# Small heads in the second attention: values as 32-column weights, a transposed result, and the exponent per head straight from PSUM

## The chip, the cores and the metric

The kernel runs on one core of a Trainium2 chip. The metric is the device time of one execution in microseconds (us). The kernel before took 516.53 us in the median of three runs (513.0 to 519.35).

## The reference, cut to what matters

The program is a decoder of four gated blocks, each an attention over a context of 128 tokens and a feed-forward part, on a batch of 8 items of 128 tokens by 128 features. Only the second attention (layer A1 in the kernel) changes. It has 16 heads of 8 features:

```
Q = split_heads(x_norm @ w_q.T); K = split_heads(ctx @ w_k.T); V = split_heads(ctx @ w_v.T)
scores = Q K^T / sqrt(8);  scores = where(mask == 0, -1e9, scores)
attn = softmax(scores, axis=-1)          # 16 heads, 128 x 128 each, per item
out  = (attn @ V) -> 128 x 128;  x = x + tanh(g) * (out @ w_o.T + b_o)
```

## The kernel before, in words

**Tiles and layers.** Everything is fp32 in tiles of 128 partitions. The program walks a plan of steps. In the first half of the plan the layers A0 (attention with 16 heads of 64 features), F0 (a quantized feed-forward part), A1 and ROUTE (the router of an expert layer) are in flight together: A0 starts at step 0, F0 at step 4, A1 at step 8, ROUTE at step 12, and each layer takes one new item per step. So F0's last work is in steps 11 to 13, A1 and ROUTE run together in steps 12 to 18, and from step 19 on ROUTE finishes alone. After that come the experts (MOE) and the layers A2, F2, A3, F3. A3 is an attention like A1 and is not changed.

**Order of work.** Each engine has a table `stages` that gives, for each layer, four slots of a step; in a slot stand entries such as `(1, scores, A1, 0)`: the lag in steps behind the item's first step, the function, its arguments. `walk` runs slot 0 of all layers, taking an entry of each in turn, then slot 1 and so on. Each engine executes its own list strictly in that order, and waits on semaphores (`wait`) for what it needs. A PSUM bank is taken with `claim`, which waits for the event in `emptied` that says its previous content has been read.

**A1 for one item** works on four groups g of four heads:

1. `scores` (PE, L817 and L821): adds the mask by a bf16 matmul and the scores of four heads by a 512-column fp32 matmul, which the profile shows as two instructions, into bank g % 2 (`S_BANK`).
2. `shifted` (DVE): row maximum per head (L1214), then scores minus maximum into `prob` (L1218). That second instruction frees the bank.
3. `exps` (ACT, L569): one exponent of 512 columns, in place, with the scale 8^-0.5.
4. `probsT` (PE, L829): four transposes; `probsT_sb` (ACT, L561) copies them to SBUF.
5. `pv` (PE, L847): per head the transposed probabilities are the weights (128 x 128) and 9 columns of `va_1` stream, 8 values and a column of ones that yields the softmax denominator. Each is two instructions, so 8 per group.
6. After all groups `norm` (DVE, L1252 and L1254) divides, `ot` (PE, L899) transposes the 128 x 128 result, `ot_sb` (ACT) copies it, `y` (PE, L905 and L907) multiplies by the output weights, `resid` (DVE, L1197) adds to x.

Before that stand the layer norm (`ln_stats`, `rs` on POOL, `ln`), its transpose `xt` and copy `xt_sb`, and `q` with `q_sb`, which writes the query to `qz` in four copies of 32 partitions. The transposes `xt` and `ot` share bank 6 (`R_BANK[0]`). At the program's start POOL clears constants (L451 to L457), and ACT and DVE wait for five of these (`cleared`).

## Time and profile before

| | us |
|---|---|
| median of three runs | 516.53 (513.0 to 519.35) |
| profiled execution, its own time | 514.63 |
| its span in the trace | 512.8 |
| PE, PEld, DVE, ACT, POOL busy in the span | 430.0, 338.2, 336.4, 275.1, 141.6 |

PE is the matrix engine and PEld its weight load, which overlaps it; DVE is the vector engine, ACT the scalar engine. The span is the stretch from the first to the last recorded instruction; the rest of the execution's time lies around it. A busy time is the sum of an engine's instructions with overlaps counted once. PE's instructions are pipelined: the next one starts before the last one's recorded end, so the cost of one in a row of equal ones is the distance between starts.

### The profile page before, as it was taken

The page shows a single profiled execution, that of the slowest core. Times are in us where ns is not written, and L with a number is a line of the kernel's source. Part 1 is how long each engine was busy: PE and PEld are TensorE (multiplying, and loading weights), DVE is VectorE, ACT ScalarE, POOL GpSimd, SP SyncE. Part 2 cuts the span into 40 slices and gives each one's busy share as a digit, 9 for nine tenths or more (in the row PEclk, how much of TensorE's full clock was granted, in tenths as well). Part 3 has the DMA queues.
Part 4 walks back from the last instruction along what each step waited for, and adds up shares of the span by engine and source line. Part 5 has one row for each costly group of instructions (what it writes and reads, how often), then busy time and mean ns, then how long its engine had stood idle before and what let it go on. Part 6 is the DMA issues. An engine that isn't in the chain of part 4 may idle for free.

```text
span 512.8 us, 8536 instructions
## 1 busy us (share of the span) xinstructions
PE 430.0 (84%) x2872; PEld 338.2 (66%) x2886; DVE 336.4 (66%) x1001; ACT 275.1 (54%) x565; POOL 141.6 (28%) x257
## 2 busy tenths in 40 slices
PE   5799899898897789889996799727779999999733
PEld 4587787787786566667786488515556777777722
DVE  1386876886976867757876122236757677888674
ACT  3343345454455356645562265323877889888553
POOL 3180010010120222204434300078552234442252
PEclk9999999999999999979998699955999999999655
DMA  8970000000000020000000223111000000000000
GB/s 312 411 283 2 1 1 2 1 1 1 1 3 0 1 106 20 1 0 12 12 17 20 88 78 116 43 36 37 11 1 2 2 1 0 2 6 6 7 10 15
DMA packets 8570, 21.41 MB, mean 42 GB/s; under 512 B 1376, under 2 KB 4689, under 8 KB 8401
## 3 DMA queue, kind: packets, MB, share of 16 engines
q1 hardware_dynamic: 7505, 18.78, 10.3%
q0 software_dynamic: 1024, 2.10, 1.4%
q8 instruction: 24, 0.39, 0.3%
q14 instruction: 17, 0.14, 0.1%
HBM read 14.00 MB, written 6.88 MB: 41 GB/s over the span
## 4 chain that ended last, share of the span: by engine, by line
PE 65%; DVE 15%; ACT 7%; issue 6%; POOL 6%; DMA 2%; POOLq 0%; DVEq 0%; ACTq 0%; another core or an unknown queue 0%
PE bank L821 9%; PE bank L847 8%; PE bank L829 7%; PE bank L866 4%; PE bank L843 4%; PE bank L805 3%; PE bank L861 3%; PE bank L984 3%; PE bank L992 3%; PE bank L946 2%; PE bank L957 2%; POOL moe_rows L528 2%; PE bank L935 2%; PE bank L788 2%; DVE prob L1218 2%
## 5 line engine op out<-in xcount | busy, mean ns | idle before, releaser
L1214 DVE TENSOR_REDUCE mx<-bank 128x4 f32<-128x512 f32 x96 | 65.8, 685 | 45.3 <-PE bank L821 29.7
L479 POOL TENSOR_SCALAR rstd<-mv 128x1 f32<-128x1 f32 x48 | 10.1, 211 | 241.7 <-DVE mv L1174 240.3
L561 ACT ACTIVATE probT<-bank 128x512 f32<-128x512 f32 x96 | 56.9, 592 | 34.0 <-PE bank L829 31.7
L569 ACT ACTIVATE prob<-prob 128x512 f32<-128x512 f32 x96 | 60.0, 625 | 25.7 <-DVE prob L1218 25.1
L847 PEld LDWEIGHTS bank<-va,probT 128*128 128x128 f32 x512 | 65.8, 199 | 3.0 <-issue 2.9
L1218 DVE TENSOR_TENSOR prob<-bank,mx 128x512 f32<-128x512 f32 x96 | 65.3, 681 | 1.6 <-PE bank L829 0.3
L829 PE MATMUL bank<-pack,prob 128*128 128x128 f32 x384 | 59.8, 279 | 5.2 <-ACT sg L637 1.4
L847 PE MATMUL bank<-va,probT 128*128 128x9 f32 x512 | 63.8, 252 | 0.3
L829 PEld LDWEIGHTS bank<-pack,prob 128*128 128x128 f32 x384 | 46.7, 147 | 25.5 <-issue 22.2
L821 PE MATMUL bank<-moe_rows,qz 128*128 128x512 f32 x64 | 34.2, 618 | 0.1
L821 PE MATMUL bank<-kz,qz 128*128 128x512 f32 x64 | 32.6, 599 | 1.4 <-issue 1.4
L843 PE MATMUL bank<-va,probT 128*128 128x65 f32 x256 | 32.1, 268 | 0.1
L843 PEld LDWEIGHTS bank<-va,probT 128*128 128x128 f32 x256 | 31.3, 192 | 0.0
L528 POOL DMA_INDIRECT moe_rows<-yrows_d,row_of x16 | 15.8, 985 | 48.4 <-DMA yrows_d<-o_n 44.6
L481 POOL TENSOR_TENSOR rstd<-rstd,minus_half 128x1 f32<-128x1 f32 x48 | 26.9, 560 | 4.0
L561 ACT ACTIVATE qT<-bank 128x512 f32<-128x512 f32 x24 | 14.3, 596 | 17.1 <-PE bank L866 17.0
L561 ACT ACTIVATE xnT<-bank 128x128 f32<-128x128 f32 x32 | 8.7, 273 | 26.7 <-PE bank L788 26.7
L866 PEld LDWEIGHTS bank<-xnT,pack 128*128 128x128 f32 x128 | 16.6, 192 | 6.2 <-issue 5.5
L866 PE MATMUL bank<-pack 128*128 128x128 f32 x128 | 18.1, 285 | 2.9 <-ACT kz L561 2.9
L523 POOL DMA_INDIRECT xrows_d<-xn_all,row_of x16 | 16.3, 1017 | 14.8 <-DVE row_of L1378 12.4
L805 PEld LDWEIGHTS bank<-kz,qT 64*128 64x128 f32 x256 | 15.5, 187 | 6.8 <-issue 6.8
L1189 DVE TENSOR_SCALAR xn<-pack,mv,rstd 128x128 f32<-128x128 f32 x40 | 13.8, 357 | 8.9 <-POOL rstd L481 8.7
(230 smaller groups left out, 944.9 us busy)
## 6 DMA issues: line engine op xcount, KB each, us to landing
yrows_d<-moe_rows SPq DMA_DIRECT2D x2, 1510.0 KB, 19.2
pack<-pack_d SPq DMA_DIRECT2D x5, 512.0 KB, 8.2
pack<-pack_d SPq DMA_DIRECT2D x1, 2112.0 KB, 14.8
expert<-experts_d SPq DMA_DIRECT2D x4, 514.0 KB, 9.2
pack<-experts_d SPq DMA_DIRECT2D x4, 514.0 KB, 4.6
xrows_d<-moe_rows SPq DMA_DIRECT2D x1, 1080.0 KB, 17.9
moe_rows<-xrows_d SPq DMA_DIRECT2D x8, 135.0 KB, 3.0
yrows_d<-o_n SPq DMA_DIRECT2D x8, 135.0 KB, 1.8
```

The costliest lines, as they stand in the source:

```text
L481: pool.tensor_tensor(out, out, minus_half, ALU.pow).then_inc(ev.sem, 1)
L528: pool.indirect_dma_start(y_got[:, b, j, :], None, yrows_d, bass.IndirectOffsetOnAxis(ap=row_of[:, b, j:j + 1], axis=0)).then_inc(y_fetche ...
L561: act.activation(dst, src, ACT.Identity if kw else ACT.Copy, **kw).then_inc(E[layer][name].sem, 1)
L569: act.activation(prob[:, g % 2, :], prob[:, g % 2, :], ACT.Exp, scale=float(DK0 if layer == A0 else DK) ** -0.5).then_inc(E[layer]["probs" ...
L805: mm_ = pe.matmul(bank[S_BANK[a]][:, P * t:P * t + P], qT[rows, it.k, cols], kz[rows, it.k, cols], start=False, stop=(t == 3))
L821: mm_ = pe.matmul(out[:, :], qz[:, it.k, P * g:P * g + P], k4[layer][:, it.b % K4_BUFS[layer], :], start=neg is None, stop=True)
L829: mm_ = pe.transpose(bank[T_BANK[g % 2]][:, P * j:P * j + P], prob[:, g % 2, P * j:P * j + P], ident)
L843: mm_ = pe.matmul(bank[O_BANK[g % 2]][:, VW0 * j:VW0 * j + VW0], probT[:, g % 2, P * j:P * j + P], va0[:, it.k, h, :], start=True, stop=True)
L847: mm_ = pe.matmul(bank[O_BANK[it.k]][:, VW * h:VW * h + VW], probT[:, g % 2, P * j:P * j + P], va[:, bass.ds(it.b, 1), h, :], start=True, ...
L866: mm_ = pe.matmul(out[:, P * t:P * t + P].rearrange("p (a n) -> p a n", a=1), w[:, 512 * c + P * t:512 * c + P * t + P], rhs, start=True, ...
L1214: yield from do(dve.tensor_reduce(m, src, AX.X, ALU.max))
L1218: yield from do(dve.tensor_tensor(prob[:, g % 2, :].rearrange("p (h t) -> p h t", h=GH), src, m.rearrange("p (h a) -> p h a", a=1).to_broa ...
```

## The change

The values of A1 are no longer the streamed operand. They are kept with each head in a field of 32 columns (`VSTEP`; 8 values and 24 zeros), and `pv` loads a window of 32 columns as weights and streams the 128 columns of the transposed probabilities. The window starts 8 g columns early, so that the head's values fall on output rows 8 g to 8 g + 7 of the strip of 32 partitions that belongs to j; the four groups accumulate in one 128 x 128 block of PSUM, which is the result already transposed. The column of ones goes away: the exponent, now four instructions per group that read the scores from PSUM with minus the maximum as bias, gives the denominators by its sum output. The subtraction on DVE goes away, and a small negation of the maxima comes. The query takes over the scale 8^-0.5. `norm1` (DVE) forms the reciprocals spread to 128 columns, `rt` (PE) transposes them, `rt_sb` (ACT) copies them, `scale1` (DVE) multiplies the result by them. The transpose of the result (`ot`) and its copy fall away. The wide values lie in a free half of `kz` and in a new tile `hi_1`, which POOL clears at the start. The rows of the output weights are reordered on the host.

```diff
-        va_1 = sb("va_1", [P, B, H, VW])
+        hi_1 = sb("hi_1", [P, B // 2 * H * VSTEP])
+        kz0 = kz[:, 0, :].rearrange("p (k n) -> p k n", k=2)
+        va_1 = [v.rearrange("p (b h n) -> p b h n", b=B // 2, h=H) for v in (kz[:, 1, :], hi_1[:, :])]
+        for g in range(G):
+            emptied[A1, f"s{g}"] = ("probs", g + 1)
 # POOL
+            pool.memset(kz[:, 1, :], 0.0).then_inc(cleared, 1)
+            pool.memset(hi_1[:, :], 0.0).then_inc(cleared, 1)
 # ACT
+            def exps1(it, g):
+                wait(act, A1, "shifted", it, 2 * g + 2)
+                if g >= 2 or it.rep >= 1:
+                    wait(act, A1, "probsT", it, g - 1)
+                for j in range(GH):
+                    ins = act.activation(prob[:, g % 2, P * j:P * j + P], bank[S_BANK[g % 2]][:, P * j:P * j + P], ACT.Exp,
+                                         bias=mxn[:, g % 2, j:j + 1],
+                                         accum_out=rden[:, it.k, G * j + g:G * j + g + 1])
+                ins.then_inc(E[A1]["probs"].sem, 1)
+            def rt_sb(it):
+                wait(act, A1, "ot", it)
+                evac(xn_all[:, it.b, :], bank[R_BANK[0]][:, 0:P], A1, "ot_sb")
-                A1: [[(2, exps, A1, 3), (2, probsT_sb, A1, 2)],
-                     [(3, ot_sb, A1), (1, exps, A1, 0), (2, probsT_sb, A1, 3)],
-                     [(1, exps, A1, 1), (1, probsT_sb, A1, 0), (0, xt_sb, A1)],
-                     [(1, exps, A1, 2), (1, probsT_sb, A1, 1), (0, q_sb, A1)]],
+                A1: [[(2, exps1, 3), (2, probsT_sb, A1, 2)],
+                     [(1, exps1, 0), (2, probsT_sb, A1, 3)],
+                     [(1, exps1, 1), (1, probsT_sb, A1, 0), (0, xt_sb, A1), None, (2, rt_sb)],
+                     [(1, exps1, 2), (1, probsT_sb, A1, 1), (0, q_sb, A1)]],
 # PE
+                    elif layer == A1:
+                        at = VSTEP * (H * (it.b % (B // 2)) + h) - DK * g
+                        mine = (kz[:, 1, :], hi_1[:, :])[it.b // (B // 2)]
+                        mm_ = pe.matmul(bank[O_BANK[it.k]][VSTEP * j:VSTEP * j + VSTEP, 0:P], mine[:, at:at + VSTEP],
+                                        probT[:, g % 2, P * j:P * j + P], start=(g == 0), stop=(g == G - 1))
+            def rt(it):
+                wait(pe, A1, "norm", it, 1)
+                claim(it, A1, "ot")
+                pe.transpose(bank[R_BANK[0]][:, 0:P], xn_all[:, it.b, :], ident).then_inc(E[A1]["ot"].sem, 1)
-                A1: [[(1, scores, A1, 0), (2, probsT, A1, 2), (2, pv, A1, 1), (3, ot, A1)],
+                A1: [[(1, scores, A1, 0), (2, probsT, A1, 2), (2, pv, A1, 1)],
                      [(1, scores, A1, 1), (2, probsT, A1, 3), (2, pv, A1, 2), (3, y, A1)],
-                     [(1, scores, A1, 2), (1, probsT, A1, 0), (2, pv, A1, 3), (0, xt, A1)],
+                     [(1, scores, A1, 2), (1, probsT, A1, 0), (2, pv, A1, 3), (0, xt, A1), (2, rt)],
 # DVE
+            def shifted1(it, g):
+                wait(dve, A1, "scores", it, g + 1)
+                do = chain(A1, "shifted", it, 2 * g)
+                src = bank[S_BANK[g % 2]][:, :].rearrange("p (h t) -> p h t", h=GH)
+                yield from do(dve.tensor_reduce(mx[:, g % 2, :], src, AX.X, ALU.max))
+                if g >= 2 or it.rep >= 1:
+                    wait(dve, A1, "probs", it, g - 1)
+                yield from do(dve.tensor_scalar(mxn[:, g % 2, :], mx[:, g % 2, :], -1.0, None, ALU.mult), hold=False)
+            def norm1(it):
+                wait(dve, A1, "probs", it)
+                dve.reciprocal(xn_all[:, it.b, :].rearrange("p (h n) -> p h n", h=H), rden[:, it.k, :].rearrange(
+                    "p (h a) -> p h a", a=1).to_broadcast([P, H, DK])).then_inc(E[A1]["norm"].sem, 1)
+            def scale1(it):
+                wait(dve, A1, "ot_sb", it)
+                wait(dve, A1, "pv", it)
+                dve.tensor_tensor(oT[:, it.k, 0:P], bank[O_BANK[it.k]][:, 0:P], xn_all[:, it.b, :], ALU.mult
+                                  ).then_inc(E[A1]["norm"].sem, 1)
-                A1: [[[(1, shifted, A1, 0), (0, ln_stats, A1)]],
-                     [[(1, shifted, A1, 1), (0, ln, A1)], (3, resid, A1)],
-                     [(1, shifted, A1, 2)],
-                     [[(1, shifted, A1, 3), (2, norm, A1)]]],
+                A1: [[[(1, shifted1, 0), (0, ln_stats, A1)], (2, norm1)],
+                     [[(1, shifted1, 1), (0, ln, A1)], (3, resid, A1)],
+                     [(1, shifted1, 2)],
+                     [(1, shifted1, 3), (2, scale1)]],
```

## Rows read from the trace of the kernel before

**Rows 1.** The page: busy times, PE in 40 slices, chain by engine.
```profile
PE 430.0 (84%) x2872; PEld 338.2 (66%) x2886; DVE 336.4 (66%) x1001; ACT 275.1 (54%) x565; POOL 141.6 (28%) x257
...
PE   5799899898897789889996799727779999999733
...
PE 65%; DVE 15%; ACT 7%; issue 6%; POOL 6%; DMA 2%; POOLq 0%; DVEq 0%; ACTq 0%; another core or an unknown queue 0%
```
**Rows 2.** Busy time by stretch, steps 11, 12 and 14: stretch, length, engines, PE's clock.
```profile
195.90:209.70 13.80, 11.99 (x80) 9.00 (x80) 11.07 (x31) 8.46 (x20) 2.59 (x5) 1.00 0.00 1
209.70:224.80 15.10, 12.67 (x81) 9.42 (x80) 10.88 (x27) 8.19 (x19) 2.83 (x5) 0.94 0.00 1
...
238.10:248.80 10.70, 10.70 (x75) 8.40 (x74) 8.42 (x26) 6.40 (x15) 4.48 (x8) 1.00 0.04 13
```
**Rows 3.** Timeline of PE in step 14: start us, length, instruction, count.
```profile
239.16 0.38 PE L817 MATMUL bank<-neg,identb 128*128 128x512 bf16 x1
239.38 1.02 PE L821 MATMUL bank<-moe_rows,qz 128*128 128x512 f32 x2
...
240.38 0.63 PE L829 MATMUL bank<-pack,prob 128*128 128x128 f32 x4
240.85 0.96 PE L847 MATMUL bank<-va,probT 128*128 128x9 f32 x8
241.66 0.31 PE L899 MATMUL bank<-pack,o_n 128*128 128x128 f32 x1
```
**Rows 4.** Timeline of PE in a step of A0: a tiled run and its neighbours.
```profile
100.77 1.06 PE L866 MATMUL bank<-xnT,pack 128*128 128x128 f32 x8
101.67 1.00 PE L843 MATMUL bank<-va,probT 128*128 128x65 f32 x8
...
105.98 0.59 PE L797 MATMUL bank<-neg,identb 128*128 128x512 bf16 x2
106.50 1.16 PE L805 MATMUL bank<-kz,qT 64*128 64x128 f32 x16
107.60 0.39 PE L935 MATMUL bank<-t_upT,xqT 128*128 128x512 bf16 x1
```
**Rows 5.** Timeline of ACT: an exponent with bias and sum, then copies.
```profile
378.70 0.37 ACT L601 ACTIVATE va<-bank,va 128x128 f32<-128x128 f32 x1
378.96 0.19 ACT L601 ACTIVATION_READ_ACCUMULATOR va<-bank,va 128x1 f32 x1
379.06 1.50 ACT L561 ACTIVATE qz<-bank,pack 32x128 f32<-32x128 f32 x4
```
**Rows 6.** Groups by line on ACT and DVE: count, busy us, mean ns.
```profile
L569 ACT ACTIVATE prob<-prob 128x512 f32<-128x512 f32 x96 | 60.0, 625 | 25.7 <-DVE prob L1218 25.1
L1218 DVE TENSOR_TENSOR prob<-bank,mx 128x512 f32<-128x512 f32 x96 | 65.3, 681 | 1.6 <-PE bank L829 0.3
L1241 DVE RECIPROCAL rden<-bank 128x4 f32<-128x4 f32 x32 | 5.7, 178 | 17.6 <-PE bank L843 17.6
L1252 DVE RECIPROCAL rden<-bank 128x16 f32<-128x16 f32 x16 | 3.9, 243 | 1.1 <-PE bank L847 1.1
```
**Rows 7.** Timeline of step 11: ACT's exponents and copies, DVE's chain of F0.
```profile
199.01 0.69 ACT L561 ACTIVATE hid<-bank,qs 128x512 f32<-128x512 f32 x1 [0.55 <-PE bank L935]
199.60 0.62 ACT L569 ACTIVATE prob<-prob 128x512 f32<-128x512 f32 x1
...
200.54 0.66 DVE L1293 SCALAR_TENSOR_TENSOR hid<-sg,hid 128x512 f32<-128x512 f32 x1
...
201.48 0.69 DVE L1214 TENSOR_REDUCE mx<-bank 128x4 f32<-128x512 f32 x1 [0.28 <-PE bank L821]
...
205.40 0.14 DVE L1283 TENSOR_SCALAR qs<-qs 128x1 f32<-128x1 f32 x1
```
**Rows 8.** The chain that ended last, in step 11: start us, length, link.
```profile
208.35 0.68 ACT hqT L561
209.03 0.52 ACT prob L569
209.55 0.61 ACT sg L623
```
**Rows 9.** Timeline of the start: POOL's last clearing, and the first data.
```profile
2.18 2.66 POOL L457 MEMSET moe_rows<- 128x3072 f32 x1
```

More of the change, by code:

```diff
@@ L62 @@
 TERNARY = ["gateT", "upT", "downT", "fcT", "projT", "w1T", "w2T"]
+VSTEP = 32
 class Item:
@@ L215, in build @@
         kT_1 = sb("kT_1", [P, B, P])
-        kT_3 = sb("kT_3", [P, B, P])
-        va_1 = sb("va_1", [P, B, H, VW])
+        hi_1 = sb("hi_1", [P, B // 2 * H * VSTEP])
+        kT_3 = hi_1[:, 0:N].rearrange("p (b t) -> p b t", b=B)
         va_3 = sb("va_3", [P, B, H, VW])
@@ L256, in build @@
         mx = sb("mx", [P, 2, GH])
+        mxn = sb("mxn", [P, 2, GH])
         rden = sb("rden", [P, 2, H])
@@ L453, in _ @@
                 pool.memset(va0[:, k, :, DK0:VW0], 1.0).then_inc(cleared, 1)
-            for va in (va_1, va_3):
-                pool.memset(va[:, :, :, DK:VW], 1.0).then_inc(cleared, 1)
+            pool.memset(kz[:, 1, :], 0.0).then_inc(cleared, 1)
+            pool.memset(hi_1[:, :], 0.0).then_inc(cleared, 1)
+            pool.memset(va_3[:, :, :, DK:VW], 1.0).then_inc(cleared, 1)
             pool.memset(qz[:, :, :], 0.0).then_inc(cleared, 1)
@@ L578, in k_sb @@
                 wait(act, A0, "kps", it, c + 1)
-                evac(kz[:, it.k, 512 * c:512 * c + 512], bank[R_BANK[0]][:, :], A0, "k_sb")
+                evac(kz0[:, it.k, 512 * c:512 * c + 512], bank[R_BANK[0]][:, :], A0, "k_sb")
             def q_sb0(it, c):
@@ L589, in q_sb @@
                     mine = slice(GH * DK * g, GH * DK * g + GH * DK)
-                    kw = dict(bias=col["bq_3"][mine]) if layer == A3 else {}
+                    kw = dict(bias=col["bq_3"][mine]) if layer == A3 else dict(scale=float(DK) ** -0.5)
                     evac(qz[mine, it.k, P * g:P * g + P], bank[R_BANK[1]][mine, 0:P], layer, "q_sb", **kw)
@@ L686, in kv_sb @@
                 else:
-                    act.activation(va[:, half, :, 0:DK], bank[c][:, :].rearrange("p (b h n) -> p b h n", b=4, h=H),
+                    dst = va[:, half, :, 0:DK] if n else va[c % 2][:, :, :, 0:DK]
+                    act.activation(dst, bank[c][:, :].rearrange("p (b h n) -> p b h n", b=4, h=H),
                                    ACT.Copy).then_inc(kv_act, 1)
@@ L732, in _ @@
             act.wait_ge(prep_dve, 1)
-            act.wait_ge(cleared, 5)
+            act.wait_ge(cleared, 6)
             prepare()
@@ L804, in row_scores0 @@
                         rows = slice(64 * a, 64 * a + 64)
-                        mm_ = pe.matmul(bank[S_BANK[a]][:, P * t:P * t + P], qT[rows, it.k, cols], kz[rows, it.k, cols],
+                        mm_ = pe.matmul(bank[S_BANK[a]][:, P * t:P * t + P], qT[rows, it.k, cols], kz0[rows, it.k, cols],
                                         start=False, stop=(t == 3))
@@ L844, in pv @@
                                         va0[:, it.k, h, :], start=True, stop=True)
+                    elif layer == A1:
[3 more added lines that the diff above has]
+                                        probT[:, g % 2, P * j:P * j + P], start=(g == 0), stop=(g == G - 1))
                     else:
-                        va = va_1 if layer == A1 else va_3
                         mm_ = pe.matmul(bank[O_BANK[it.k]][:, VW * h:VW * h + VW], probT[:, g % 2, P * j:P * j + P],
-                                        va[:, bass.ds(it.b, 1), h, :], start=True, stop=True)
+                                        va_3[:, bass.ds(it.b, 1), h, :], start=True, stop=True)
                 mm_.then_inc(E[layer]["pv"].sem, 1)
@@ L905, in y @@
                 pe.matmul(out, ones, col[f"bo_{n}"], start=True, stop=False)
-                wait(pe, layer, "ot_sb", it)
+                wait(pe, layer, "norm" if layer == A1 else "ot_sb", it)
                 pe.matmul(out, oT[:, it.k, mine_of(layer)], col[f"woT_{n}"], start=False, stop=True).then_inc(E[layer]["y"].sem, 1)
@@ L1024, in kv3 @@
                     if c < 2:
-                        wait(pe, A1, "shifted", last)
+                        wait(pe, A1, "probs", last)
                     else:
@@ L1118, in piece_name @@
                     return args[0]
-                return {xt_e: "xt", down: "y", y_back: "yb", places: "places", y0: "y", q: "q", ot: "ot", y: "y", scores2: "s", probsT2: "t", pv2: "pv", ht: "ht",
+                return {xt_e: "xt", down: "y", y_back: "yb", places: "places", y0: "y", q: "q", ot: "ot", rt: "ot", y: "y", scores2: "s", probsT2: "t", pv2: "pv", ht: "ht",
                         y_ffn: "y", logits: "lg"}[fn]
@@ L1481, in prepare @@
                                          ALU.mult, ALU.min).then_inc(prep_dve, 1)
-                dve.wait_ge(cleared, 5)
+                dve.wait_ge(cleared, 6)
                 dve.wait_ge(gates_ready, 1)
```

2 lines of the change are left out of this document (1 added, 1 removed).

## The prediction

> **What bounds the kernel now.** I read the page first: PE is busy for 430.0 of 512.8 us and holds 65% of the chain that ended last, DVE 15%, ACT 7% [rows 1]. That is an average, so the stage of the change was read next, step by step. A1 shares steps 9 to 12 with F0 and steps 13 to 16 with ROUTE. The reader should see two regimes [rows 2]. In step 14 PE is busy 10.70 of 10.70 us and ACT 6.40: PE alone sets the step. In steps 11 and 12 PE is busy 11.99 of 13.80 and 12.67 of 15.10 us; nothing is full there, and the step is a chain through PE, DVE and ACT [rows 7, 8]. A change that moves work from DVE to ACT and recasts PE's work has to be priced in both.
>
> **PE: the eight instructions of a group's `pv`.** Before, they take from 240.85 to 241.66, 0.81 us, or 0.10 each: the load of 128 columns of weights sets that pace, not the 9 streamed columns [rows 3]. After, each streams 128 columns of fp32. At full array that is the pace of L866, eight in 0.90 us (100.77 to 101.67), 0.11 each [rows 4]. So without overlap the swap gains nothing. But the four heads go to four strips of columns. The trace has one case of a divided array, L805, where two strips of 64 rows alternate: 16 instructions of the same 128 streamed columns in 1.16 us, the last recorded 0.285 long, so 0.058 apart [rows 4]. Two instructions per head must follow each other in one strip, and instructions start in order, so four strips give the same picture as two: pair by pair, half the time. I take 0.058 x 8 = 0.47 us. The division has a price at its edges: L797 streams until 106.40 (2 x 0.21), L805 starts at 106.50; it streams until 107.43, the next whole-array instruction starts at 107.60: 0.10 + 0.17 = 0.27 us [rows 4]. A group costs 0.74 us, 0.07 less than now; over 32 groups 2.2 us. Bounds: no overlap of column strips 8 x 0.11 + 0.27 = 1.15 us (32 x 0.34 = 11 us more), full overlap of four strips 2 x 0.11 + 0.27 = 0.49 (32 x 0.32 = 10 us less).
>
> The Trainium skill (TensorEngine Tiling (Array Packing), Performance Considerations) recommends exactly this swap of stationary and streaming operand with column tiling, at up to 4x for 32; its Tiling Modes section says that changing the mode drains the engine. The edge gaps above agree with the second; the 4x would be the low bound, and it is the first rival.
>
> `rt` takes the place of `ot`, one transpose of 128 columns for another; zero. But it stands right behind `xt` in slot 2 and both use bank 6, so `rt` must wait until ACT has copied `xt`.
>
> **ACT: the exponent.** The nearest row is L601, a 128x128 exponent from PSUM with bias and sum: it starts at 378.70, its accumulator read at 378.96, the next instruction at 379.06: 0.36 us each [rows 5]. A group takes 4 x 0.36 = 1.44 us, where one of 0.625 stood, which in a row with others costs 0.52 [rows 6, 8]: 0.92 more, 3.7 us per item, 29 us in all eight. It is the same operation, so the bounds are narrow (0.30 to 0.45 each). `rt_sb` replaces `ot_sb`, zero; the scaled `q_sb` stays a copy of the same shape, zero. ACT in step 14 goes from 6.40 to 10.1 us of work, against PE's 10.70 - 4 x 0.07 = 10.4: two engines nearly full at once, each waiting in order on the other.
>
> **DVE.** It loses 4 x 0.681 us per item, at a pace of 0.60 [rows 6], and gets four negations of 128x4. The nearest is 0.14 for 128x1 [rows 7]; with the hold behind the reduce I take 0.25. `norm1` is a reciprocal of 128 columns. From 4 to 16 columns the time grows 65 ns, 5.4 ns a column [rows 6], which gives 0.243 + 112 x 5.4 ns = 0.85 us; low bound 0.28, as if it streamed like a plain operation. Net -2.4 + 1.0 + 0.6 = -0.8 us of work. `scale1` is like the multiply of `norm`. DVE is not full in either regime, so only its place in the chain counts.
>
> **Waits.** The score bank is now freed by the exponent, not by the subtraction. From maximum to probabilities it was 0.60 + 0.63; it is 0.25 + 1.44, 0.5 us longer, and `scores` g + 2 stands behind it on PE, with `probsT` and `pv` behind that. `norm1` in DVE's slot 0 waits for the exponent of group 3 in ACT's slot 0, and behind it on DVE stands slot 1: F0's `hid0`, which is on the chain, the next maximum and `ln`.
>
> **Steps 10 to 12 (with F0).** In step 11 the copy `up_sb` ends on ACT at 199.60 and the exponent of group 3 follows [rows 7]. It will end at 201.05, `norm1` at about 201.95, and F0's first `hid` then starts at 202.0 in place of 200.54; `scores` 1 starts at 201.1, so its maximum comes near 202.65, not 201.48: 1.2 us later. The subtraction gone from the chain gives back 0.5. So F0's quantized rows come 0.7 later, `hqT` too. Then on the chain hqT, prob, sg [rows 8] the exponent of 0.52 becomes 1.44: 0.9. Together 1.6 us a step, three steps, 4.8 us. Step 9 has only the last term without `norm1`: 0.9 - 0.4 = 0.5.
>
> **Steps 13 to 16 (with ROUTE).** I walked one step from the start of `scores` 0. PE: scores 1.08, logits 0.2, transposes 0.44, pv 0.74, at 2.45; slot 1 (scores, transposes, pv, y, places) ends at 5.3. ACT: rest of the query copies 0.87 and exponent 3 end at 2.3, copy 2.8, exponent 0 4.25, copy 4.75, exponent 1 6.2, so no bank is late so far. Slot 2 on PE: scores and transposes end at 6.95, pv and `xt` at 7.75. ACT copies the transposes until 7.65, `xt` until 8.2; `rt` can start only then (PE idle 0.4), its copy ends at 8.8, and exponent 2, behind it, runs until 10.25; copy 10.75, first query copy 11.05. The next step starts there: 11.05 in place of 10.70, and with a hand-over or two not counted 11.2. Four steps, 2.0 us.
>
> **Tail and start.** Behind the last `pv` the transpose and its copy fall away (0.31 [rows 3] and a copy of about as much), 0.6 us less in step 17. At the start POOL clears 2 x 2048 columns more; 3072 take 2.66 us [rows 9], so 3.5 us. The constants that ACT waits for are then ready near 5.6 us, when the first data land anyway; the 3072 columns end near 8.2, in front of SP's store that starts at 7.4, whose data are wanted only by the router. Zero; if that cover were gone, 0.1 to 1.
>
> **Sum.** 4.8 + 0.5 + 2.0 - 0.6 = +6.7 us on the profiled execution's 514.63: 521.3. The median of the runs stands 1.9 above that execution; I put the forecast between, at 522.
>
> **Rivals.**
>
> 1. *Full overlap of four strips, and PE stays the only bound.* Then every group saves 0.32 us: 516.5 - 10 = 506. For: PE sets step 14 alone. Against: pairs in one strip must follow one another, and ACT's 10.1 us of step 14 allow hardly 0.6 us of gain. Chance 0.12.
> 2. *Slower by more: column strips do not overlap.* L805 divides rows, where each strip reads its own partitions; here all strips stream different data over the same 128 partitions. Place: `pv`, 32 times. Price 8 x (0.11 - 0.058) = 0.42 us a group, 13 us where PE counts, some 10 with the slack of steps 10 to 12: 532. It decides as soon as starts inside `pv` are 0.1 apart. Chance 0.18.
> 3. *The longer exponent falls into ACT's idle time.* ACT idles 13.80 - 8.46 = 5.3 us in step 11 and 4.3 in step 14 [rows 2]; if order lets it, only PE's 2.2 us remain, minus: 514. Against: the chain names ACT's exponent in step 11 [rows 8]. Chance 0.15.
>
> The forecast has 0.55, its own range 514 to 530 (a reciprocal of 0.28 us takes 2 off, exponents at 0.30 or 0.45 move it by 6 either way over the chain's steps, and a step at PE's lower clock, such as the 0.94 of step 12 [rows 2], adds some).
>
> **Numbers.** A change of 2% (506.2 or 526.9) is about what can be told from none. Faster: 0.10 of rival 1 and 0.02 of rival 3, 0.12. Slower: 0.17 of rival 2 and 0.13 of the forecast's upper end, 0.30. Within: 0.58. The range 507 to 534 holds all but the low tail of rival 1 and the ends.
>
> **What would show it.** In the trace after: `pv` starts 0.06 apart (0.03 for rival 1, 0.11 for rival 2) and gaps of some 0.27 around them; four exponents of 0.36 each; the reciprocal near 0.85; step 14 at 11.2 with both PE and ACT above 90%; PE idle before `rt`; step 11 at 15.4, with `hid` behind `norm1`. What would make it wrong: the wait of `norm1` hidden, since the exponent of group 3 came earlier; or the clock of PE falling in steps that now have gaps, which would cost several us at once.

## The result, and the profile after

The changed kernel takes 518.5 us in the median of 19 runs (516.26 to 522.28), the kernel before 514.35 us (511.11 to 520.35) in as many on the same chip: a ratio of 1.0086, 95% interval 1.0062 to 1.011. It is slower by 0.9%, some 4.4 us, and lies within 2%. The forecast was 522, its working +6.7 us.

First the page of the changed kernel, as in [rows 1]: busy times, PE and its clock in 40 slices, the chain by engine.

```profile
PE 423.0 (82%) x2872; PEld 316.1 (61%) x2886; DVE 326.1 (63%) x1001; ACT 300.9 (58%) x789; POOL 143.6 (28%) x258
...
PE   5799899889887878688886699827779999999733
...
PEclk9999999999999898989998599965899999999755
...
PE 56%; DVE 17%; ACT 13%; issue 7%; POOL 5%; DMA 2%; another core or an unknown queue 0%; POOLq 0%; DVEq 0%; ACTq 0%
```

PE lost 7.0 us of work and DVE 10.3, and ACT gained 25.8. The chain lost PE (65% to 56%) and took up DVE and ACT. The kernel does less matrix work in more time (its span is 3.8 us longer), so PE stands idle for some 11 us more.

Next the busy times by stretch of the changed kernel. A stretch is a step, from one `q` to the next: steps 9 to 14. [Rows 2] has steps 11, 12 and 14 of before.

```profile
159.48:179.55 20.07, 16.05 (x100) 12.08 (x100) 11.67 (x39) 11.94 (x41) 2.66 (x5) 0.93 0.00 1
179.55:197.27 17.72, 14.19 (x95) 8.97 (x96) 10.50 (x31) 12.01 (x48) 2.48 (x5) 0.89 0.29 91
197.27:211.89 14.62, 10.80 (x80) 6.22 (x80) 9.47 (x29) 11.29 (x47) 2.48 (x5) 1.00 0.00 0
211.89:228.13 16.24, 12.03 (x80) 6.72 (x79) 9.40 (x26) 11.75 (x49) 2.48 (x5) 0.89 0.01 2
228.13:239.27 11.14, 9.78 (x79) 5.90 (x78) 7.12 (x28) 9.16 (x42) 4.66 (x7) 1.00 0.04 13
239.27:250.42 11.15, 9.77 (x76) 5.70 (x75) 7.13 (x26) 9.38 (x45) 4.53 (x7) 1.00 0.04 13
```

And the same view of the kernel before, steps 10 and 13:

```profile
179.70:195.94 16.24, 13.52 (x96) 10.68 (x96) 11.05 (x30) 8.28 (x19) 2.59 (x5) 1.00 0.27 99
...
224.77:238.13 13.36, 13.36 (x79) 10.54 (x78) 8.79 (x28) 6.24 (x15) 4.65 (x7) 0.81 0.02 6
```

In step 14 PE was busy all 10.70 us; now 9.77 of 11.15. The following table puts one profiled execution of each kernel side by side. "Next part" is the start of the first 128x512 projection behind A1 and the router (L1009 before, L1042 after), from PE's timeline; "tail" is what lies between step 15 and it.

| us | before | after | difference | forecast |
|---|---|---|---|---|
| up to the end of step 9 | 179.70 | 179.55 | -0.15 | +0.5 |
| steps 10 to 12 | 45.07 | 48.58 | +3.5 | +4.8 |
| steps 13 to 15 | 34.77 | 33.43 | -1.3 | +1.5 |
| tail | 26.64 | 28.68 | +2.0 | -0.1 (+0.5 - 0.6) |
| next part starts at | 286.18 | 290.24 | +4.06 | +6.7 |

Behind that point the two take 226.6 and 226.4 us, so the whole difference lies ahead of it. The -1.3 is one step: step 13 of before took 13.36 us at a granted clock of 0.81 and busy throughout, against 11.14 at 1.00. Steps 14 and 15 are 0.44 us longer each.

PE's timeline of the changed kernel in step 14, to set beside [rows 3]:

```profile
241.95 0.43 PE L872 MATMUL bank<-probT,hi 128*32 128x128 f32 x8
242.69 0.39 PE L841 MATMUL bank<-neg,identb 128*128 128x512 bf16 x1 [0.32 <-ACT prob L586]
...
244.30 0.42 PE L872 MATMUL bank<-probT,hi 128*32 128x128 f32 x8
244.66 0.49 PE L938 MATMUL bank<-pack 128*128 128x128 f32 x2
...
248.77 0.30 PE L927 MATMUL bank<-pack,xn_all 128*128 128x128 f32 x1 [0.46 <-ACT xnT L570]
248.91 0.38 PE L841 MATMUL bank<-neg,identb 128*128 128x512 bf16 x1
```

All eight instructions of `pv` lie inside 0.42 us, and the next instruction follows 0.36 us after the first (244.30 to 244.66). Before it was 0.81, and the working took 0.74. The same view, ended at 244.43, shows which of them start together:

```profile
244.30 0.32 PE L872 MATMUL bank<-probT,hi 128*32 128x128 f32 x4
```

Four have started by then, and they end within 0.32 us though each lasts 0.30. The single records give the starts as 0, 7, 13 and 20 ns, then 133, 140, 147 and 153 ns. Since instructions in one strip start 0.109 us apart (the first experiment), this is one instruction in each of the four strips and then the second one in each. All 32 groups of the trace show this pattern; in the last two, in the tail at a low clock, the second round comes after 215 ns. PE really is relieved by 0.45 us a group, 14 us in all. It pays them back as waits: for the exponent, because that now frees the score bank (0.32), and for `rt` behind `xt` (0.46).

The groups of the new instructions on ACT and DVE in the changed kernel, steps 9 to tail:

```profile
L586 ACT ACTIVATE prob<-bank,mxn 128x128 f32<-128x128 f32 x128 | 45.3, 376 | 13.6 <-DVE mxn L1263 13.5
L586 ACT ACTIVATION_READ_ACCUMULATOR prob<-bank,mxn 128x1 f32 x128 | 27.7, 216 | 0.0
...
L1267 DVE RECIPROCAL xn_all<-rden 128x128 f32<-128x128 f32 x8 | 7.6, 946 | 4.6 <-ACT prob L586 4.5
```

In a row the exponents start 0.34 to 0.35 us apart, four in 1.4 us. The reciprocal takes 0.95 us.

The chain of waits of the changed kernel in step 11, as in [rows 8]:

```profile
200.68 1.50 ACT prob L586 x8
...
202.21 0.95 DVE xn_all L1267
203.16 0.39 DVE hid L1347
...
209.88 0.50 ACT hqT L570
...
210.79 1.25 ACT prob L586 x7
212.03 0.31 ACT sg L646
```

And the chain in the tail of the changed kernel:

```profile
270.49 1.36 ACT prob L586 x7
271.86 0.62 ACT probT L570
272.47 1.40 ACT prob L586 x8
273.90 0.95 DVE xn_all L1267
...
275.31 0.25 DVE topi L1414 x2
275.70 1.09 PE bank L853 x4
```

In step 11 the last group's exponent, the reciprocal and F0's `hid` follow each other, as the working had it. In the tail the same pair, exponent then reciprocal, stands ahead of the router's `choose` (its `topi`). PE, which before went on to these transposes without a gap, waits, and does its last work at a lower clock (0.71 granted from 274 to 278 us): from the first of four transposes to the next instruction it is 1.02 us instead of 0.44. The wait is in PE's timeline:

```profile
275.70 1.09 PE L853 MATMUL bank<-pack,prob 128*128 128x128 f32 x4 [2.37 <-DVE topi L1414]
```

### The profile page after: what moved, and what is told of

The parts are those of the page before. It is cut to its first block, busy times and chain, and to the rows that moved or that the text cites. A ratio compares the mean times of both kernels' runs of the same rounds, so it can differ in the third digit from the quotient of the medians.

```text
span 516.6 us, 8793 instructions
## 1 busy us (share of the span) xinstructions
PE 423.0 (82%) x2872; PEld 316.1 (61%) x2886; DVE 326.1 (63%) x1001; ACT 300.9 (58%) x789; POOL 143.6 (28%) x258
## 3 DMA queue, kind: packets, MB, share of 16 engines
q1 hardware_dynamic: 7505, 18.78, 10.3%
## 4 chain that ended last, share of the span: by engine, by line
PE 56%; DVE 17%; ACT 13%; issue 7%; POOL 5%; DMA 2%; another core or an unknown queue 0%; POOLq 0%; DVEq 0%; ACTq 0%
PE bank L845 7%; PE bank L853 5%; PE bank L894 4%; PE bank L875 4%; ACT prob L586 4%; PE bank L867 4%; PE bank L829 3%; PE bank L889 3%; PE bank L1017 3%; PE bank L1025 3%; PE bank L979 2%; PE bank L968 2%; PE bank L990 2%; POOL moe_rows L537 2%; PE bank L904 1%
## 5 line engine op out<-in xcount | busy, mean ns | idle before, releaser
L586 ACT ACTIVATE prob<-bank,mxn 128x128 f32<-128x128 f32 x128 | 45.3, 376 | 13.6 <-DVE mxn L1263 13.5
L1251 DVE TENSOR_TENSOR prob<-bank,mx 128x512 f32<-128x512 f32 x64 | 43.9, 686 | 1.3 <-PE bank L853 0.3
L578 ACT ACTIVATE prob<-prob 128x512 f32<-128x512 f32 x64 | 39.9, 623 | 5.6 <-DVE prob L1251 5.4
L845 PE MATMUL bank<-moe_rows,qz 128*128 128x512 f32 x64 | 35.8, 643 | 0.8 <-ACT qz L570 0.8
L875 PEld LDWEIGHTS bank<-va,probT 128*128 128x128 f32 x256 | 33.4, 199 | 3.0 <-issue 2.9
L875 PE MATMUL bank<-va,probT 128*128 128x9 f32 x256 | 32.1, 253 | 0.3
L867 PEld LDWEIGHTS bank<-va,probT 128*128 128x128 f32 x256 | 31.3, 192 | 0.0
L586 ACT ACTIVATION_READ_ACCUMULATOR prob<-bank,mxn 128x1 f32 x128 | 27.7, 216 | 0.0
```

The costliest lines, as they stand in the source:

```text
L578: act.activation(prob[:, g % 2, :], prob[:, g % 2, :], ACT.Exp, scale=float(DK0 if layer == A0 else DK) ** -0.5).then_inc(E[layer]["probs" ...
L586: ins = act.activation(prob[:, g % 2, P * j:P * j + P], bank[S_BANK[g % 2]][:, P * j:P * j + P], ACT.Exp, bias=mxn[:, g % 2, j:j + 1], acc ...
L845: mm_ = pe.matmul(out[:, :], qz[:, it.k, P * g:P * g + P], k4[layer][:, it.b % K4_BUFS[layer], :], start=neg is None, stop=True)
L867: mm_ = pe.matmul(bank[O_BANK[g % 2]][:, VW0 * j:VW0 * j + VW0], probT[:, g % 2, P * j:P * j + P], va0[:, it.k, h, :], start=True, stop=True)
L875: mm_ = pe.matmul(bank[O_BANK[it.k]][:, VW * h:VW * h + VW], probT[:, g % 2, P * j:P * j + P], va_3[:, bass.ds(it.b, 1), h, :], start=True ...
L1251: yield from do(dve.tensor_tensor(prob[:, g % 2, :].rearrange("p (h t) -> p h t", h=GH), src, m.rearrange("p (h a) -> p h a", a=1).to_broa ...
```

## The experiments

**Do the strips overlap, and was that all of PE's gain?** All heads of a group go to strip 0, with each product written over the last instead of accumulated.

```diff
-pe.matmul(bank[O_BANK[it.k]][VSTEP * j:VSTEP * j + VSTEP, 0:P], mine[...], probT[...], start=(g == 0), stop=(g == G - 1))
+pe.matmul(bank[O_BANK[it.k]][0:VSTEP, 0:P], mine[...], probT[...], start=True, stop=True)
```

> The kernel after with all heads of a group written to the first strip of 32 partitions, without accumulation (the result is left wrong: three quarters of it are never written), so that the eight instructions can't overlap across strips. If the 0.35 us of a group come from four strips at once: eight instructions about 0.11 apart, 0.86 us and the edges, 0.5 us more a group; steps 14 and 15 go from 11.15 to about 12, the time 5 to 12 us above the kernel after. If they come from the small weights alone: 0.35 us a group as before, no change from the kernel after.

Measured: 523.56 us, ratio 1.0158 (1.011 to 1.0207). PE's timeline of this kernel in step 14, and the stretch:

```profile
243.47 1.06 PE L872 MATMUL bank<-probT,hi 128*32 128x128 f32 x8
244.46 0.39 PE L841 MATMUL bank<-neg,identb 128*128 128x512 bf16 x1
```

```profile
240.37:252.81 12.44, 11.98 (x76) 8.21 (x75) 7.07 (x26) 9.61 (x45) 4.55 (x7) 1.00 0.03 11
```

The next instruction follows after 0.99 us instead of 0.36. Same instructions, same shapes, another strip: the overlap of the four strips is worth 0.63 us a group. The eight starts are 0.109 us apart here, each behind the last. The step is 1.3 us longer, not 2.5, since a part went into waits that PE has anyway. This kernel is the world of the second rival, column strips that don't overlap: 523.56 us where the rival said 532, and only 0.7% above the changed kernel (four runs, and the two intervals nearly touch).

**The exponent by itself.** The kernel before with `exps1` and `shifted1` alone; the sums go to a tile that nobody reads.

```diff
+                    ins = act.activation(prob[:, g % 2, P * j:P * j + P], bank[S_BANK[g % 2]][:, P * j:P * j + P], ACT.Exp,
+                                         bias=mxn[:, g % 2, j:j + 1], accum_out=sums1[:, it.k, G * j + g:G * j + g + 1])
-                A1: [[(2, exps, A1, 3), (2, probsT_sb, A1, 2)],
+                A1: [[(2, exps1, 3), (2, probsT_sb, A1, 2)],
```

> The kernel before with the new exponent alone (four exponents per group from PSUM with bias and sum, negated maxima on DVE); values product and normalization as before. Theory A (the exponent costs the chain 0.9 us in steps 9 to 12 and, with PE at its full 10.7 us of work in steps 13 to 16, every wait for a bank shows): 5 to 10 us above the kernel before (ratio 1.01 to 1.02), more than the whole change. Theory B (it falls into ACT's idle time): ratio 0.995 to 1.002.

Measured: 510.72 us, ratio 0.9935 (0.9903 to 0.9966). The part that I had priced as the loss is a small gain, below both ranges that I had given. The stretch of step 14 in this kernel:

```profile
236.65:247.31 10.66, 10.66 (x75) 8.46 (x74) 6.59 (x26) 9.40 (x45) 4.53 (x7) 1.00 0.05 15
```

ACT went from 6.40 to 9.40 us, PE is still busy without a gap, and DVE has 1.8 us less to do. While PE sets the step, the longer exponent is free. In steps 10 to 12 it is not: they take 46.53 us against 45.07, step 10 of them at a clock of 0.91. Step 11 ran at full clock in both kernels, and there the exponent alone costs 0.70 us (14.47 against 13.77):

```profile
197.22:211.69 14.47, 12.13 (x81) 8.99 (x81) 8.49 (x31) 11.78 (x49) 2.96 (x5) 1.00 0.00 0
```
 Where all of the 0.65% comes from I can't say: in the trace 2.5 us are step 13, which here ran at full clock (10.89 against 13.36), and 2.3 us lie in stages behind (224.3 us after 226.6), which the edit doesn't touch.

**The same question inside the changed kernel.** One exponent of 512 columns per group from PSUM, with the first head's bias and without sums; the reciprocal and its transpose stay.

```diff
-                for j in range(GH):
-                    ins = act.activation(prob[..., P * j:P * j + P], bank[...][:, P * j:P * j + P], ACT.Exp, bias=mxn[:, g % 2, j:j + 1], accum_out=...)
+                ins = act.activation(prob[:, g % 2, :], bank[S_BANK[g % 2]][:, :], ACT.Exp, bias=mxn[:, g % 2, 0:1])
```

> The exponent of a group is one instruction of 512 columns from PSUM with the bias of the group's first head and without sums; the path of the normalization stays. So ACT gives back 1.40 - 0.6 = 0.8 us a group. Theory (the chain through normalization ends the steps, and the exponent is a link of it in steps 10 to 12 and in the tail): 0.8 us in each of steps 10 to 12, some 0.4 in each of 13 to 15, 1 to 1.6 in the tail, 5 to 7 us less, ratio 0.995 to 0.999. Rival (ACT's longer exponent is in idle time, the normalization alone costs): at most 1.5 us less, ratio 1.005 to 1.009.

Measured: 510.61 us, ratio 0.988 (0.9824 to 0.9935), more than either side had expected. The stretches of steps 12 and 14 in it:

```profile
210.31:224.18 13.87, 10.65 (x80) 6.12 (x79) 9.11 (x26) 8.47 (x19) 3.05 (x5) 1.00 0.01 1
...
234.60:245.02 10.42, 9.84 (x75) 5.60 (x74) 7.12 (x26) 6.67 (x15) 4.53 (x7) 1.00 0.05 17
```

Against the changed kernel: steps 10 to 12 -3.5 us, steps 13 to 15 -0.7 each, tail -2.3, the next part at 281.81 instead of 290.24. So the same four exponents that cost nothing beside the old PE work are 2% here by the ratios. A part of that is the clock: steps 10 and 12 of the changed kernel ran at 0.89 and here at 1.00 (step 11 the other way round, 1.00 and 0.89), and runs at like clock, in the part on the prediction, give some 6 us, 1.2%. At full clock in both traces stand the 0.7 us of each of steps 13 to 15. With `pv` at 0.36 us and the normalization waiting for their end, PE no longer covers the exponents.

**The path of the normalization, taken out.** The same edit on two kernels: on the changed one, and on one that has the new `pv` with the old subtraction and exponent. There the denominators are missing; this second base is the first run below, and the two after it also leave the division out. (`...` stands for entries that don't change.)

```diff
-                A1: [[[(1, shifted1, 0), (0, ln_stats, A1)], (2, norm1)],
+                A1: [[[(1, shifted1, 0), (0, ln_stats, A1)]],
-                     [..., (0, xt_sb, A1), None, (2, rt_sb)],
+                     [..., (0, xt_sb, A1)],
-                     [..., (0, xt, A1), (2, rt)],
+                     [..., (0, xt, A1)],
-                dve.tensor_tensor(oT[:, it.k, 0:P], bank[O_BANK[it.k]][:, 0:P], xn_all[:, it.b, :], ALU.mult
+                dve.tensor_tensor(oT[:, it.k, 0:P], bank[O_BANK[it.k]][:, 0:P], ones, ALU.mult
```

> The kernel after with the old softmax back (maximum and subtraction on DVE, one exponent of 512 columns per group on ACT) and the new values product kept. It leaves the softmax denominators out: the reciprocal is taken of old numbers. Theory A (the values product now costs PE 0.35 us a group where it cost 0.81, 15 us in all, and what eats that gain is the exponent): steps 13 to 16 fall from 10.7 to about 9.2 us, steps 10 to 12 by about 0.5, and the time is 6 to 10 us below the kernel before (ratio 0.98 to 0.988). Theory B (the swap itself gains nothing, because the steps are chains and not PE's work): ratio 0.995 to 1.005.

> e1 without the normalization path: no reciprocals, no transpose rt, no copy rt_sb; the product is multiplied by ones, so the division by the denominators is left out. The swap alone in e1 took 1.2% more than the kernel before although PE's product fell from 0.81 to about 0.4 us a group. Theory C (the new normalization path, with its 0.95 us reciprocal on DVE and its hand-overs through bank 6, is what the swap pays with): steps 14 and 15 fall from 11.3 to about 9.3 us, and the time is 5 to 10 us below the kernel before (ratio 0.98 to 0.99). Theory D (the divided array is what costs, by its mode changes and by PE's lower clock in steps 9 to 12): steps 14 and 15 fall, steps 9 to 12 stay at 17 us with a clock of 0.8 to 0.9, ratio 1.00 to 1.01.

> The kernel after without the normalization path (no reciprocals, no rt, no rt_sb; multiplied by ones, the division is left out); exponents with their sums kept. Theory C: the waits of PE behind the copy of xt (0.46 and 0.61 us a step) and of DVE behind the exponent of group 3 go, steps 14 and 15 fall from 11.15 to about 10 (ACT's 9.4 us of work are then the floor), the ratio to the kernel before is 0.985 to 0.995. Theory D: ratio 1.00 to 1.01.

| | with the path | without | the path |
|---|---|---|---|
| new `pv`, old exponent | 1.0124 (1.0076 to 1.0173) | 0.9876 (0.9834 to 0.9918) | 2.5% |
| new `pv`, new exponent | 1.0086 (1.0062 to 1.011) | 0.984 (0.98 to 0.9879) | 2.5% |

The first of these kernels took 522.20 us, 1.2% more than before: neither of my two theories for it came (0.98 to 0.988, 0.995 to 1.005). The other two took 509.43 and 507.49 us, as the theory of the path had it, and against the rival that the divided array itself costs; only step 14 fell less than I had said (to 10.55 and 10.41 us, not 9.3 and 10). Three instructions, a reciprocal, a transpose and a copy, 1.5 us of work per item, cost 11 to 13 us over eight items. Both rows say the same, so it doesn't hang on the exponent's form. In the traces of the second row the next part starts 11.7 us earlier: 3.1 us of that are step 10, 0.5 step 11, 2.5 step 12, 2.2 steps 13 to 15 and 3.5 the tail. Step 12 is mostly clock: it ran at 0.89 with the path and 1.00 without. Both kernels without the path also had the higher clock over their whole runs (0.917 to 0.933 against 0.899 to 0.920); whether the path brings the lower clock is not shown. The stretches of steps 11 and 14 in the changed kernel without the path:

```profile
194.29:208.42 14.13, 10.56 (x80) 6.12 (x79) 8.36 (x30) 11.61 (x48) 2.97 (x5) 1.00 0.00 1
...
232.54:242.95 10.41, 9.46 (x74) 5.54 (x73) 6.71 (x25) 9.12 (x44) 4.54 (x7) 1.00 0.06 20
```

Step 14 gives back 0.74 us, as with the single exponent (0.73): in slot 2 ACT's exponent and the hand-over of `rt` follow each other, and either one gone frees the same time. The tail is 25.22 us instead of 28.68.

**Place or length of the reciprocal?** First `norm1` a slot later, then the reciprocal taken of 16 columns and spread by a copy, then both.

```diff
-                A1: [[[(1, shifted1, 0), (0, ln_stats, A1)], (2, norm1)],
-                     [[(1, shifted1, 1), (0, ln, A1)], (3, resid, A1)],
+                A1: [[[(1, shifted1, 0), (0, ln_stats, A1)]],
+                     [[(1, shifted1, 1), (0, ln, A1)], (3, resid, A1), (2, norm1)],
```

```diff
-                dve.reciprocal(xn_all[...], rden[...].to_broadcast([P, H, DK])).then_inc(E[A1]["norm"].sem, 1)
+                dve.reciprocal(rden[:, it.k, :], rden[:, it.k, :]).then_inc(E[A1]["norm"].sem, 1)
+                dve.wait_ge(E[A1]["norm"].sem, E[A1]["norm"].at(it, 1))
+                dve.tensor_copy(xn_all[...], rden[...].to_broadcast([P, H, DK])).then_inc(E[A1]["norm"].sem, 1)
```

> The kernel after with the reciprocal (norm1) moved on DVE from the end of slot 0 to the end of slot 1, behind F0's first hidden operation and the next maximum. If norm1, which waits for the exponent of group 3 and then takes 0.95 us, holds back F0's chain in steps 10 to 12: 2 to 4 us less than the kernel after (ratio to the kernel before 1.001 to 1.005). If the maximum behind it waits for the same exponent through its bank anyway: no change from the kernel after (1.007 to 1.011).

> The reciprocal is taken of the 128x16 denominators and spread to 128 columns by a copy, so that norm1 should hold DVE for some 0.24 + 0.25 with a hold between, 0.55 to 0.6 us, in place of 0.95. Theory (the length of norm1 ahead of hid0 and, in the tail, ahead of choose is on the path): up to 0.35 to 0.4 us in each of steps 10 to 12 and once an item in the tail, 1.5 to 3 us less than the changed kernel, ratio 1.003 to 1.006. Rival (only its wait for the exponent of group 3 counts, not its length): no difference, ratio 1.008 to 1.010.

> The same short reciprocal, and norm1 behind slot 1 instead of slot 0 of DVE. Theory: the gains of the two add as far as they touch the same steps; norm1 a slot later gave 0.5%, and its length then stands ahead of fewer things, so ratio 0.999 to 1.003. Rival (once norm1 stands behind hid0 its length is in DVE's idle time): the same as norm1 one slot later alone, 1.003 to 1.005.

Measured: later 1.0038 (1.001 to 1.0067), short 0.9976 (0.9939 to 1.0012), both 1.0 (0.9964 to 1.0036). The place came as the first theory had it. Shortening an instruction of 0.95 us is worth 1.1%, more than I had expected, and moving it behind as well adds nothing that the intervals show. DVE's timeline in step 11 of the kernel with the short reciprocal:

```profile
201.21 0.25 DVE L1267 RECIPROCAL rden<-rden 128x16 f32<-128x16 f32 x1 [1.03 <-ACT prob L586]
201.50 0.23 DVE L1269 COPY xn_all<-rden 128x128 f32<-128x128 f32 x1
201.64 0.68 DVE L1349 SCALAR_TENSOR_TENSOR hid<-sg,hid 128x512 f32<-128x512 f32 x1
```

`hid` starts 0.43 us after the reciprocal, not 0.95. The stretches of steps 10 to 12 there:

```profile
179.09:195.78 16.69, 12.49 (x98) 8.05 (x97) 9.45 (x32) 12.33 (x51) 2.84 (x5) 1.00 0.30 97
195.78:210.09 14.31, 10.85 (x82) 6.22 (x80) 8.85 (x32) 11.80 (x49) 2.84 (x5) 1.00 0.00 0
210.09:224.04 13.95, 10.64 (x80) 6.11 (x79) 8.11 (x27) 11.37 (x48) 2.70 (x5) 1.00 0.01 2
```

Step 11, at full clock in both traces, is 0.31 us shorter: that is the length on the chain. Steps 10 and 12 are 1.0 and 2.3 us shorter, and PE is busy 1.7 and 1.4 us less in them for the same instructions: in the changed kernel they ran at a clock of 0.89. So most of the gain in this pair of traces is the clock. How much of it is in the 1.1% of the timed runs stays open, since the runs' own clocks by step aren't recorded; runs at like mean clock, below, give 0.6%. The tail stays at 28.56, but it ran at a granted clock of 0.73 against 0.81 of the changed kernel, so it can't be read for the length. PE's wait in it did get shorter, 1.99 us instead of 2.37:

```profile
271.79 1.09 PE L853 MATMUL bank<-pack,prob 128*128 128x128 f32 x4 [1.99 <-DVE topi L1416]
```

The place counts for more: with `norm1` a slot later `choose` runs ahead of the reciprocal, the wait is 0.59 us, and the tail is 26.20, with both edits 25.81 (at clocks of 0.85 and 0.84).

**Can the order of `rt` be mended?** `rt` ahead of `xt` on PE, and its copy ahead of `xt_sb` on ACT.

```diff
-                     [(1, exps1, 1), (1, probsT_sb, A1, 0), (0, xt_sb, A1), None, (2, rt_sb)],
+                     [(1, exps1, 1), (1, probsT_sb, A1, 0), None, (2, rt_sb), (0, xt_sb, A1)],
-                     [(1, scores, A1, 2), (1, probsT, A1, 0), (2, pv, A1, 3), (0, xt, A1), (2, rt)],
+                     [(1, scores, A1, 2), (1, probsT, A1, 0), (2, pv, A1, 3), (2, rt), (0, xt, A1)],
```

> The transpose rt stands ahead of xt on PE, and its copy ahead of xt_sb on ACT. Theory (the hand-over through bank 6 costs PE 0.46 us per step before rt, since rt waits for the copy of xt): rt no longer waits for ACT, xt waits for the copy of rt instead, so steps 13 to 15 stay within 0.3 us of 11.15; the two share one bank in either order, and the ratio stays 1.006 to 1.011. Rival (the wait is one of order alone and can be removed by order): steps 13 to 15 fall to 10.7, ratio 1.003 to 1.005.

Measured: 1.0112 (1.0076 to 1.0148). PE's timeline in step 14:

```profile
252.58 0.30 PE L927 MATMUL bank<-pack,xn_all 128*128 128x128 f32 x1 [0.62 <-ACT xnT L570]
253.34 0.30 PE L812 MATMUL bank<-pack,xn 128*128 128x128 f32 x1 [0.46 <-ACT xn_all L570]
```

The wait of 0.46 us has changed its owner, and step 14 stays at 11.16. The ratio lies just above the upper end of what I expected; in its trace step 10 ran at a clock of 0.83 and took 20.41 us. Two results through one bank and one copying engine wait for each other in either order.

**Denominators without the path.** The old way got them as a ninth streamed column for nothing. In the new layout they can come from PE too: behind each product a second one with a 32-column window of ones (8 ones, 24 zeros) as weights gives the denominator of the head already on its 8 rows, so nothing has to be spread or transposed. DVE then takes one reciprocal of a 128 x 128 block and multiplies. Both blocks accumulate in one bank, which a bf16 product with zeros clears first.

```diff
+                        pe.matmul(bank[O_BANK[it.k]][:, 0:2 * P], identb[:, :], zerob[:, :], start=True, stop=False)
...
+                        mm_ = pe.matmul(bank[O_BANK[it.k]][VSTEP * j:VSTEP * j + VSTEP, P:2 * P], ones8[:, 24 - DK * g:24 - DK * g + VSTEP],
+                                        probT[:, g % 2, P * j:P * j + P], start=False, stop=(g == G - 1))
...
+                yield from do(dve.reciprocal(rinv[:, it.k, :], bank[O_BANK[it.k]][:, P:2 * P]))
```

> A complete kernel: the new values product, the old softmax path, and the denominators from PE, by a second product per head with a window of ones as the 32-column weights and the same streamed probabilities, so that they come already spread over the result's layout; no transpose of reciprocals and no copy of it. Theory A: a group's two products cost PE about 0.57 us against 0.81, and two of the waits go; the 128-column reciprocal of 0.95 us stands on DVE behind the last product. 4 to 8 us below the kernel before (ratio 0.984 to 0.992). Theory B (only the chain through ACT and DVE counts): ratio 0.995 to 1.005.

> A complete kernel: e5 (new product, denominators by a window of ones on PE) with the new exponent from PSUM, without its sums. e2 and e5 alone stand at 0.9935 and 0.9986 of the kernel before. If the two gains add up because they are on different engines (DVE loses the subtraction, PE 0.12 us a group): 0.985 to 0.993, below e2. If PE's lower clock in the steps with gaps takes it back: 0.995 to 1.005.

Measured: with the old subtraction and exponent 514.59 us, 0.9986 (0.995 to 1.0023); with the new exponent, without sums, 508.15 us, **0.9847 (0.9813 to 0.9881)**. The first came as its theory B had it, with steps 11 and 12 at clocks of 0.89 and 0.90; the second at the lower end of the gain that I had expected. It computes all that the reference asks and beats both kernels; its steps 9 to 15 all ran at full clock in the trace. Its step 14, PE's timeline, one group's exponents on ACT, and the stretch:

```profile
235.99 0.45 PE L880 MATMUL bank<-probT,hi 128*32 128x128 f32 x8
236.23 0.42 PE L882 MATMUL bank<-probT,ones 128*32 128x128 f32 x8
236.58 0.39 PE L847 MATMUL bank<-neg,identb 128*128 128x512 bf16 x1
```

```profile
236.74 1.14 ACT L593 ACTIVATE prob<-bank,mxn 128x128 f32<-128x128 f32 x4
```

```profile
233.18:243.38 10.20, 10.20 (x108) 6.50 (x107) 7.57 (x26) 8.06 (x26) 4.54 (x7) 1.00 0.05 16
```

Both products of a group take 0.59 us, still less than the 0.81 of before. PE is busy throughout again and the waits are gone. ACT has 8.06 us instead of 9.38: the copy of `rt` is worth 0.26 of that (9.12 us in the changed kernel without the path), and the rest is the accumulators that are no longer read, four exponents in a row taking 1.14 us, not 1.40.

## Why the prediction was right, and by which of its steps

The sign, the size class and two of the mechanisms held. The sum was 2.6 us above what the profiled executions show (+4.06 up to the next part), and that nearness is luck in part: a gain of 14 us of PE's work was not foreseen, most of it went into waits that the working had not counted either, and the clock moved single steps by 2 us in both kernels.

**`pv` on PE: the saving was wrong by a factor of six.** I gave a group 0.74 us, 0.07 less than before; it takes 0.36, 0.45 less. The step that failed is "four strips give the same picture as two: pair by pair, half the time". The second instruction of a head doesn't hold up the next strip: four instructions start within 20 ns, so one in each of the four strips, and the four second ones from 133 ns on. Eight in one strip start 0.109 us apart, so a round of four strips costs about what one instruction costs, and the pace is the 2 x 0.11 of the full-overlap bound. The rest, 0.36 - 0.22 = 0.14 us by that estimate, is the edges; I had read 0.27 from another pair of shapes, and so even the bound of full overlap, 0.49, stood above the measurement. The Trainium skill (TensorE: Matmul & The Clock Gate, Part 3: Packing small matmuls) states that matmuls placed in different tiles of the array run at the same time, with about 4 ns of issue for each further tile. The trace agrees with the overlap; between starts in neighbouring strips it shows 7 ns.

**The first rival's price was right and its condition wrong.** The full overlap came, 14 us of PE, but "PE stays the only bound" didn't: PE was down to 9.77 of 11.15 us. The time it named, 506, is near where the kernels without the path of the normalization lie (509.43, 507.49 and 508.15).

**The exponent: right length, account right in part.** 1.40 us a group against 1.44. Exchanged alone, subtraction and exponent cost 0.70 us in step 11, at full clock on both sides; the working's term for a step with the exponent and without `norm1` was 0.5 (step 9), so that charge was about right. Yet the whole kernel with this exchange got 0.65% shorter, and no run says where all of that comes from. What the working had wrong is the place of the larger price. In the changed kernel the four are dear, 1 to 2% above a single one, in steps 13 to 15 (0.7 us each) and the tail too, for a reason that it held only in part: PE's cover was gone, by the very 0.45 us that I hadn't seen.

**Normalization in the steps with F0: the mechanism as forecast, the size too large.** In step 11 the exponent of group 3 ends at 202.18; the working had 201.05 in a step that began 1.3 us earlier, which is 202.4. Then comes the reciprocal, then `hid`. The reciprocal took 0.95 us, not 0.85. The step was to be 15.4 us, 1.6 more than before, and is 14.62, 0.85 more. Step 11 is also the one step of the three that ran at full clock in both kernels, and four kernels at full clock split its 0.85: the exponent +0.70, the path +0.49 (14.62 against 14.13), and the new `pv`, by difference, -0.34. The 3.5 us of the three steps looks nearer to the forecast 4.8 than that, but steps 10 and 12 of the changed kernel ran at a clock of 0.89, so that nearness is not the working's merit. Left out, the path gives 2.5% by the ratios: it is more than the whole loss, and most of it lies outside step 11, in step 10, in the hand-over of steps 13 to 15 and in the tail.

**Steps with ROUTE: right.** The walk gave 11.2, with PE idle for 0.4 us before `rt` and exponent 2 behind the copy of `rt`. The trace has 11.15, 0.46 us and that order. Of "PE and ACT above 90%" neither came (88% and 84%), since `pv` was shorter and ACT's work 9.4 us instead of 10.1. Over the whole stretch the trace shows a gain, because step 13 of before ran at a clock of 0.81; I had used step 14 for all four and not looked at what step 13 held.

**Tail: wrong sign.** I took off 0.6 us for the transpose and copy that fall away, and 2.0 were added. What the working left out is that the pair which it had found ahead of `hid`, exponent and reciprocal, stands once more ahead of the router's `choose` when the last items drain and nothing covers it. The tail is 26.37 us with one exponent per group and 26.20 with `norm1` one slot later. With the short reciprocal it is 28.56, at a lower clock, though PE waits 0.38 us less.

**The clock.** I had named a lower clock in steps with gaps as a risk. In the trace steps 9, 10 and 12 ran at 0.93, 0.89 and 0.89 where before only step 12 was below 1.00 (0.94). But it is not settled as an effect of the change: through step 9 the kernels with another place or length of the reciprocal and with another order of `rt` issue the same instructions as the changed one. With the reciprocal short or a slot later, or `rt` first, that step took 18.64 to 18.65 us at 1.00; in the changed kernel it took 20.07 at 0.93, and with the reciprocal both short and later 20.24 at 0.92. Between single executions a step can differ by that much.

The lower clock is therefore a rival for every ratio above. It can be held against the timed runs, whose mean clocks over the whole execution are on record. Among those at 0.915 to 0.918 the changed kernel has a median of 518.35 us (nine runs), the kernel before 514.07 (20 runs beside the experiments), the short reciprocal 515.24 (three) and the single exponent 512.01 (three). So at like clock the change still costs 4.3 us; the length of the reciprocal is worth 3.1 us (0.6%, where its theory had 1.5 to 3 us) and the four exponents 6.3 us (1.2%), where the ratios say 1.1 and 2%. These are few runs, and the mean doesn't fix the time: four runs of the changed kernel took 520.6 to 520.81 us at 0.919 and three others 516.26 to 517.93 at 0.920.

## What to carry to other kernels

When a change takes work from the engine that sets the time, ask first what that work had been covering: here 14 us came off PE, and the exponent, which had been free beside it, and a new reciprocal became the bound. Price a small instruction by what stands behind it in its queue and not only by its length, in the last items of a loop above all; before a ratio of 1% is put down to an edit, compare the granted clocks on both sides; and keep a by-product such as a softmax denominator in the layout in which it will be used, even at the price of one more product on PE.

## What the runs showed of the hardware

- Eight fp32 instructions with 32 columns of weights and 128 streamed columns, two in each of four column strips, occupy PE for 0.36 us; in one strip 0.99 us. Sixteen take 0.59 us. At full clock the first ones of the four strips start 7 ns apart and the second ones 0.13 us after them.
- A reciprocal on DVE takes 0.95 us for 128 columns and 0.25 for 16, so some 6.3 ns for each further column; a multiply of 128 columns takes 0.29. Where the same value is wanted many times, divide first and spread by a copy (0.25 + 0.23 us).
- An exponent of 128x128 from PSUM with bias and sum costs 0.35 us in a row, and 0.26 without the sum (four in 1.14 us, (1.14 - 0.376) / 3 between starts), so a sum costs 0.09 us.
- In steps 10 and 12, with the same instructions on PE, a granted clock of 0.89 instead of 1.00 went with 1.4 to 1.7 us more of PE's busy time (the changed kernel against the short reciprocal).
